# Expert layer of a decoder: weights as the stationary operand, rows added straight into the output

## The reference

```python
def moe(x, gate_w, w1, w3, w2):          # E = 8 experts, F = 512, TOPK = 2
    xt = x.reshape(b * s, d)             # 2048 tokens, d = 256
    logits = xt @ gate_w
    topv, topi = jax.lax.top_k(logits, TOPK)
    probs = jax.nn.softmax(topv, axis=-1)
    w = jnp.zeros_like(logits)
    for kk in range(TOPK):
        w = w + jax.nn.one_hot(topi[:, kk], E, dtype=logits.dtype) * probs[:, kk:kk + 1]
    out = jnp.zeros_like(xt)
    for e in range(E):
        h = jax.nn.silu(xt @ w1[e]) * (xt @ w3[e])
        out = out + w[:, e:e + 1] * (h @ w2[e])
    return out.reshape(b, s, d)

out = h + moe(rmsnorm(h, norm2_w), gate_w, w1, w3, w2)
```

## Time and profile before

| | us |
|---|---|
| median of 3 runs | 1277.4 (1275.44 to 1280.86) |
| the profiled execution's own time | 1279.25 |
| its span | 1277.2 |
| busy in the span: TensorE matmul / weight loads | 1159.9 / 816.0 |
| VectorE / ScalarE / GpSimd | 775.9 / 573.4 / 604.1 |
| expert stage, first row load to end | 1025.06 to 1277.2 |

### The profile page before, as it was taken

How to read it: one execution, slowest core, us unless ns; L and a number is a source line. 1 busy time by engine, 2 the same in 40 slices (tenths; PEclk the granted TensorE clock), 3 DMA queues, 4 the chain that set the end, 5 groups by cost and what they waited for, 6 DMA issues and landing times. The chain is left out here.

```text
span 1277.2 us, 24562 instructions
## 1 busy us (share of the span) xinstructions
PE 1159.9 (91%) x7393; PEld 816.0 (64%) x7394; DVE 775.9 (61%) x1914; ACT 573.4 (45%) x1505; POOL 604.1 (47%) x752
## 2 busy tenths in 40 slices
PE   7998889879999699789999999999999579999995
PEld 5785566545555344368888888888888346666663
DVE  5565788868888599755676767776766412222221
ACT  3444766633333100056666566666665223333331
POOL 2003556526555466456666556666655213223232
PEclk9999999989999899899999999999999789999998
DMA  7000000009992030140000000000003012222223
GB/s 275 0 1 9 18 14 12 9 2 205 203 198 59 15 157 1 70 198 1 9 14 14 22 13 12 12 12 16 13 22 145 31 36 43 48 41 46 44 45 86
DMA packets 46372, 69.43 MB, mean 54 GB/s; under 512 B 4609, under 2 KB 42817, under 8 KB 45249
## 3 DMA queue, kind: packets, MB, share of 16 engines
q1 hardware_dynamic: 37152, 52.95, 15.5%
q0 software_dynamic: 7152, 9.34, 4.5%
q10 hardware_dynamic: 2000, 6.29, 1.3%
HBM read 57.12 MB, written 32.58 MB: 70 GB/s over the span
## 5 line engine op out<-in xcount | busy, mean ns | idle before, releaser
L1926 PE MATMUL ga.pkq<-ga.xnT,g.early 128*128 128x128 f32 x1280 | 156.8, 276 | 1.0 <-ACT ga.halves L1844 1.0
L1926 PEld LDWEIGHTS ga.pkq<-ga.xnT,g.early 128*128 128x128 f32 x1280 | 151.4, 193 | 9.6 <-issue 8.2
L1703 POOL TENSOR_TENSOR ga.halves<-ga.halves,g.ga_sinT 128x512 f32<-128x512 f32 x80 | 103.1, 1288 | 53.1 <-ACT ga.halves L1844 53.1
L1970 PE MATMUL ga.turn_out<-g.early,ga.aT 128*128 128x256 f32 x512 | 117.0, 382 | 0.5 <-ACT ga.aT L1866 0.5
L1851 ACT ACTIVATE ga.e<-ga.psc,ga.negmax 128x128 f32<-128x128 f32 x256 | 90.6, 366 | 48.6 <-DVE ga.negmax L1772 47.7
L1711 POOL TENSOR_TENSOR ga.kqT<-ga.by_cos,ga.halves 128x512 f32<-128x512 f32 x80 | 102.3, 1279 | 15.9 <-issue 15.9
L1970 PEld LDWEIGHTS ga.turn_out<-g.early,ga.aT 128*128 128x128 f32 x512 | 94.9, 190 | 12.3 <-ACT ga.aT L1866 0.7
L2081 DVE TENSOR_TENSOR ex.hidden<-ex.silu,ex.p 128x512 f32<-128x512 f32 x39 | 26.8, 688 | 123.6 <-PE ex.p L2134 117.2
L1759 DVE TENSOR_TENSOR ga.by_cos<-ga.pkq,g.ga_cosT 128x512 f32<-128x512 f32 x80 | 55.3, 691 | 74.2 <-PE ga.pkq L1926 43.2
L2058 POOL TENSOR_TENSOR ex.token<-ex.token_d,ex.zero 128x1 uint32<-128x1 uint32 x39 | 7.0, 180 | 154.2 <-DVE ex.y L2087 143.5
L1951 PE MATMUL ga.paT<-ga.pT,ga.v 128*128 128x512 f32 x128 | 69.2, 623 | 11.8 <-ACT ga.pT L1859 9.1
(11 more groups left out here) (292 smaller groups left out, 2623.9 us busy)
## 6 DMA issues: line engine op xcount, KB each, us to landing
mo_rows<-in_pad_rows SPq DMA_DIRECT2D x1, 18447.0 KB, 100.8
ex.row<-mo_rows SPq DMA_DIRECT2D x39, 129.0 KB, 2.0
g.spare<-in_mo_w SPq DMA_DIRECT2D x1, 4096.0 KB, 12.2
g.late<-in_mo_w SPq DMA_DIRECT2D x1, 4096.0 KB, 21.9
g.early<-in_mo_w SPq DMA_DIRECT2D x1, 4096.0 KB, 12.6
g.ctxT<-in_ctxR SPq DMA_DIRECT2D x1, 2048.0 KB, 13.2
xa.ctxT<-in_ctxT SPq DMA_DIRECT2D x16, 128.0 KB, 2.5
g.spare<-cv_rows SPq DMA_DIRECT2D x1, 2048.0 KB, 9.7
```

What stands on the lines that cost most here:

```text
L1703: nc.gpsimd.tensor_tensor(by_sin[:, par, :].rearrange("p (h t) -> p h t", h=REP), halves[:, par, :].rearrange("p (h t) -> p h t", h=REP), ...
L1926: last = nc.tensor.matmul(pkq[:, par, j * P:(j + 1) * P], w[:, q, at * P:(at + 1) * P], xnT[:, s.par, q, :], start=(q == 0), stop=(q == C ...
L1970: last = nc.tensor.matmul(pout, aT[:, h // REP, (h % REP) * P:(h % REP + 1) * P], g.ga_wo[:, h, :], start=(h == 0), stop=(h == H - 1))
```

## The change

In the experts the operands of p1 and p3 change sides. The weights become stationary and the rows xnT move, so that p1 and p3 come out transposed, as four blocks of 128 hidden channels by 128 tokens in the columns of one bank; each is eight matmuls with 128 moving columns. The stationary operand isn't addressed by a register: ScalarE copies w1 of the expert of tile t+2, and VectorE w3, into buffers of their own (`w1`, `w3`, two each, 128x1024), by a register load of the expert's number on each engine. The product of silu and p3 is written as hT at once, in two buffers. The hidden transposes, their bank and ScalarE's hT copy go, and so does the register load ahead of p1. ScalarE and VectorE begin two tiles ahead instead of one (`steps(..., 2, 1)`), and wait once for the weights to be loaded.

The kernel's output tensor gets 128 rows more (for the padding rows) and takes the place of `mo_acc`: the router's sums are stored into it, the scatter adds into it, and the copy at the end goes. The padding rows are cut off after the kernel.

```diff
-        silu, hidden = m.sb("silu", [P, F]), m.sb("hidden", [P, F])
-        hT = m.sb("hT", [P, F])
+        silu, hT = m.sb("silu", [P, F]), m.sb("hT", [P, 2, F])
+        w1, w3 = m.sb("w1", [P, 2, C * F]), m.sb("w3", [P, 2, C * F])
...
@@ sync @@
             sp.wait_ge(added, 16 * TILES)
-            sp.dma_start(g.out.rearrange("b t d -> (b t d)").rearrange("(p n) -> p n", p=P),
-                         g.acc[0:B * P, :].rearrange("t d -> (t d)").rearrange("(p n) -> p n", p=P)).then_inc(out_stored, 16)
-            sp.wait_ge(out_stored, 16)
@@ vector @@
             def step(t):
+                if t.base is None and t.n == -2:
+                    dve.wait_ge(g.mo_loaded, 16 * g.mo_loads)
                 if t.on:
                     dve.wait_ge(silu_ready, upto(t))
                     dve.wait_ge(h3_done, upto(t))
-                    if t.past(1):
-                        dve.wait_ge(h_turned, upto(t, back=1))
-                    nc.vector.tensor_tensor(hidden[:], silu[:], p3[:], ALU.mult).then_inc(hidden_ready, 1)
+                    if t.past(2):
+                        dve.wait_ge(y_done, upto(t, back=2))
+                    nc.vector.tensor_tensor(hT[:, t.par, :], silu[:], p3[:], ALU.mult).then_inc(hT_ready, 1)
+                n = t.back(-2)
+                if n.on:
+                    expert = dve.value_load(g.tile_expert[0:1, bass.ds(n.i, 1)], min_val=0, max_val=E - 1)
+                    nc.vector.tensor_copy(w3[:, n.par, :], g.mo_w3[:, bass.ds(expert, 1), :, :].rearrange("p e c f -> p (e c f)")).then_inc(w3_ready, 1)
                 b = t.back(1)
...
@@ scalar @@
                     if t.past(1):
-                        act.wait_ge(hidden_ready, upto(t, back=1))
+                        act.wait_ge(hT_ready, upto(t, back=1))
                     nc.scalar.activation(silu[:], p1[:], ACT.Silu).then_inc(silu_ready, 1)
+                n = t.back(-2)
+                if n.on:
+                    expert = act.value_load(g.tile_expert[0:1, bass.ds(n.i, 1)], min_val=0, max_val=E - 1)
+                    nc.scalar.activation(w1[:, n.par, :], g.mo_w1[:, bass.ds(expert, 1), :, :].rearrange("p e c f -> p (e c f)"), ACT.Copy).then_inc(w1_ready, 1)
                 n = t.back(-1)
...
-                if t.on:
-                    act.wait_ge(h_turned, upto(t))
-                    if t.past(1):
-                        act.wait_ge(y_done, upto(t, back=1))
-                    nc.scalar.activation(hT[:], phT[:], ACT.Copy).then_inc(hT_ready, 1)
@@ tensor @@
                 if t.on:
-                    expert = pe.value_load(g.tile_expert[0:1, bass.ds(t.i, 1)], min_val=0, max_val=E - 1)
                     pe.wait_ge(xnT_ready, upto(t))
+                    pe.wait_ge(w1_ready, upto(t))
                     if t.past(1):
                         pe.wait_ge(silu_ready, upto(t, back=1))
-                    for c in range(C):
-                        last = nc.tensor.matmul(p1[:], xnT[:, t.par, c, :], g.mo_w1[:, bass.ds(expert, 1), c, :].rearrange("p e f -> p (e f)"), start=(c == 0), stop=(c == C - 1))
+                    for f in range(4):
+                        for c in range(C):
+                            last = nc.tensor.matmul(p1[:, f * P:(f + 1) * P], w1[:, t.par, c * F + f * P:c * F + (f + 1) * P], xnT[:, t.par, c, :], start=(c == 0), stop=(c == C - 1))
                     last.then_inc(h1_done, 1)
+                    pe.wait_ge(w3_ready, upto(t))
                     if t.past(1):
-                        pe.wait_ge(hidden_ready, upto(t, back=1))
+                        pe.wait_ge(hT_ready, upto(t, back=1))
...
-                if t.on:
-                    pe.wait_ge(hidden_ready, upto(t))
-                    if t.past(1):
-                        pe.wait_ge(hT_ready, upto(t, back=1))
-                    for f in range(4):
-                        last = nc.tensor.transpose(phT[:, f * P:(f + 1) * P], hidden[:, f * P:(f + 1) * P], g.ident[:])
-                    last.then_inc(h_turned, 1)
@@ decoder, kernel @@
-        g.h, g.out = h, out
+        g.h, g.acc = h, out
...
-    out = nc.dram_tensor("out_0", (B, P, D), F32, kind="ExternalOutput").ap()
+    out = nc.dram_tensor("out_0", (B * P + P, D), F32, kind="ExternalOutput").ap()
...
-    return r.results[0]["out_0"]
+    return r.results[0]["out_0"][0:B * P].reshape(B, P, D)
```

More of the change, by code:

```diff
@@ L1411, in allocate_moe @@
     g.rows = nc.dram_tensor("mo_rows", [E * REGION + SPARE * P, ROW], F32, kind="Internal").ap()
-    g.acc = nc.dram_tensor("mo_acc", [B * P + P, D], F32, kind="Internal").ap()
     g.tile_expert, g.tile_row = m.sb("tile_expert", [P, TILES], I32), m.sb("tile_row", [P, TILES], I32)
@@ L2015, in experts @@
         xnT = m.sb("xnT", [P, 2, C, P])
-        silu, hidden = m.sb("silu", [P, F]), m.sb("hidden", [P, F])
-        hT = m.sb("hT", [P, F])
+        silu, hT = m.sb("silu", [P, F]), m.sb("hT", [P, 2, F])
+        w1, w3 = m.sb("w1", [P, 2, C * F]), m.sb("w3", [P, 2, C * F])
         y = m.sb("y", [P, 2, D])
[L2019 to L2023, removed]
+        turn, p1, p3, py = m.ps("turn", [P, 512]), m.ps("p1", [P, F]), m.ps("p3", [P, F]), m.ps("py", [P, 512])
+        (meta_ready, token_ready, turned, xnT_ready, w1_ready, w3_ready, h1_done, h3_done, silu_ready, hT_ready, y_done, y_ready,
+         added) = map(m.sem, (
+            "meta_ready", "token_ready", "turned", "xnT_ready", "w1_ready", "w3_ready", "h1_done", "h3_done", "silu_ready", "hT_ready",
+            "y_done", "y_ready", "added"))
         row_loaded = [m.sem(f"row_loaded{i}") for i in range(2)]
@@ L2092, in step @@
                     meta(n)
-            steps(dve, step, 1, 1, count=TILES)
+            steps(dve, step, 2, 1, count=TILES)
         @block.scalar
@@ L2097, in step @@
             def step(t):
+                if t.base is None and t.n == -2:
+                    act.wait_ge(g.mo_loaded, 16 * g.mo_loads)
                 if t.on:
@@ L2110, in step @@
                     last.then_inc(xnT_ready, 1)
-                if t.on:
-                    act.wait_ge(h_turned, upto(t))
-                    if t.past(1):
-                        act.wait_ge(y_done, upto(t, back=1))
-                    nc.scalar.activation(hT[:], phT[:], ACT.Copy).then_inc(hT_ready, 1)
-            steps(act, step, 1, 1, count=TILES)
+            steps(act, step, 2, 1, count=TILES)
         @block.tensor
@@ L2123, in step @@
                 if t.on:
-                    expert = pe.value_load(g.tile_expert[0:1, bass.ds(t.i, 1)], min_val=0, max_val=E - 1)
                     pe.wait_ge(xnT_ready, upto(t))
+                    pe.wait_ge(w1_ready, upto(t))
                     if t.past(1):
                         pe.wait_ge(silu_ready, upto(t, back=1))
-                    for c in range(C):
-                        last = nc.tensor.matmul(p1[:], xnT[:, t.par, c, :], g.mo_w1[:, bass.ds(expert, 1), c, :].rearrange("p e f -> p (e f)"), start=(c == 0), stop=(c == C - 1))
+                    for f in range(4):
+                        for c in range(C):
+                            last = nc.tensor.matmul(p1[:, f * P:(f + 1) * P], w1[:, t.par, c * F + f * P:c * F + (f + 1) * P], xnT[:, t.par, c, :], start=(c == 0), stop=(c == C - 1))
                     last.then_inc(h1_done, 1)
+                    pe.wait_ge(w3_ready, upto(t))
                     if t.past(1):
-                        pe.wait_ge(hidden_ready, upto(t, back=1))
-                    for c in range(C):
-                        last = nc.tensor.matmul(p3[:], xnT[:, t.par, c, :], g.mo_w3[:, bass.ds(expert, 1), c, :].rearrange("p e f -> p (e f)"), start=(c == 0), stop=(c == C - 1))
+                        pe.wait_ge(hT_ready, upto(t, back=1))
+                    for f in range(4):
+                        for c in range(C):
+                            last = nc.tensor.matmul(p3[:, f * P:(f + 1) * P], w3[:, t.par, c * F + f * P:c * F + (f + 1) * P], xnT[:, t.par, c, :], start=(c == 0), stop=(c == C - 1))
                     last.then_inc(h3_done, 1)
@@ L2150, in step @@
                     for f in range(4):
-                        last = nc.tensor.matmul(py[:, 0:D], hT[:, f * P:(f + 1) * P], g.mo_w2[:, bass.ds(expert, 1), f, :].rearrange("p e d -> p (e d)"), start=(f == 0), stop=(f == 3))
+                        last = nc.tensor.matmul(py[:, 0:D], hT[:, b.par, f * P:(f + 1) * P], g.mo_w2[:, bass.ds(expert, 1), f, :].rearrange("p e d -> p (e d)"), start=(f == 0), stop=(f == 3))
                     last.then_inc(y_done, 1)
-                if t.on:
-                    pe.wait_ge(hidden_ready, upto(t))
-                    if t.past(1):
-                        pe.wait_ge(hT_ready, upto(t, back=1))
-                    for f in range(4):
-                        last = nc.tensor.transpose(phT[:, f * P:(f + 1) * P], hidden[:, f * P:(f + 1) * P], g.ident[:])
-                    last.then_inc(h_turned, 1)
             steps(pe, step, 1, 1, count=TILES)
```

## The result

The changed kernel takes 1258.56 us (median of 4 runs, 1257.11 to 1259.13) where the kernel before takes 1276.94 beside it: ratio 0.9851, 95% interval 0.9832 to 0.9869. Forecast were 1256.6 us and a range of 1251 to 1268. A second series, run later with the experiments (e4), gave 1257.43 against 1277.93: 0.9836 (0.9823 to 0.9849). The gain is 18.4 us in the first series and 20.5 in the second, where 20.8 was forecast. The profiled execution took 1259.13 us, its span is 1257.1.

What follows compares the result with a forecast made beforehand. The prediction took TensorE's own stream to bound the turns and the output copy to bound the end. Savings of 10.5 + 0.75 + 1.15 + 8.4 = 20.8 us from the median 1277.4 gave 1256.6 us, range 1251 to 1268.

Steps and rivals of the forecast that it cites:

- point 1: TensorE's turn: p1 and p3 as 32 records of 0.1117 us, plus row transposes and py, sum 5.52 us.
- point 2: Expert-number load ahead of py on TensorE's sequencer: mostly covered by queued records, costing 0.08 us a turn.
- The rival of ample cover: TensorE's queue takes in more than 7 to 8 records, so the expert-number load costs nothing: 1253.6 us; chance 0.15.
- point 3: TensorE's loop jump, now behind py, and the dropped load for p1: the 0.14 us in every second turn goes.
- points 4 to 6: ScalarE's w1 copy (1.02 us), VectorE's w3 copy (at most about 1.22) and GpSimd's scatter chain: each cost 0.
- point 7: First turn, p1(0) to p1(1): 7.72 us becomes 6.97, saving 0.75 us.
- point 8: Last turn, p1(38) to py(38): 6.53 us becomes 5.38, saving 1.15 us.
- point 9: End of the span: the output copy goes and everything after it until 1277.2, saving 8.4 us.

Runs made afterwards that it cites:

- e4: The changed kernel unaltered, run once more beside the other experiments: 1257.43 us against 1277.93 for the kernel before, ratio 0.9836.
- e5: The changed kernel with one more load of the expert's number ahead of py on TensorE's sequencer: 1257.41 us, ratio 0.9845.
- e6: The changed kernel with three more loads of the expert's number ahead of py on TensorE's sequencer: 1305.41 us, ratio 1.0220.
- e7: The changed kernel with the w1 copy made twice on ScalarE, the second into a buffer nobody reads: 1257.93 us, ratio 0.9849.
- e8: The changed kernel with two banks for py instead of one: 1257.54 us, ratio 0.9846.
- e1: The kernel before with only the output tensor changed, rows added straight into it and no copy at the end: 1271.51 us, ratio 0.9954.
- e3: The changed kernel with GpSimd waiting for the last scatter's landing ahead of its closing drain: 1259.54 us, ratio 0.9851.
- e10: The changed kernel with a GpSimd drain in every turn, behind the token operation and ahead of the scatter: 1257.46 us, ratio 0.9838.
- e11: The changed kernel with a GpSimd drain in every turn at the head of the step, before the wait for the previous scatter: 1256.85 us, ratio 0.9827.

## Why the prediction was right, and where it was not

The time came out 2 us above the forecast and well inside the range; by the profiled executions the sum was 20.8 and the stage gave 20.6. That is closer than the working deserves, and luck: the turns gave 3.0 us more than forecast, the last turn 1.2 and the end 1.9 less, and the three nearly cancel.

- *Turn (point 1)*: right to the hundredth. 32 records at the attention stage's 0.112, transposes and py at their old price give 5.52, and 5.521 was measured. The weight loads lie beneath the matmuls at this shape in the new place too; laid end to end with the matmuls they would make a turn of over 11 us. The Trainium skill's rule that a load overlaps only with different row groups (TensorE: Matmul & The Clock Gate, "The mechanism"; the prediction names the section behind it) doesn't hold here: TensorE is busy for 204.28 of 204.28 us with all rows in use.
- *Expert number for py (point 2)*: wrong. I took 0.08 us a turn; there is none, 3.0 us in the sum. I read a depth of 7 to 8 records off the moment at which the sequencer turned to the next register load. In that turn the sequencer had been held: it stood ahead of the hidden transposes, waiting for the hidden product. In the turn whose row follows, the product ends at 1145.93 + 0.69 = 1146.62, and the sequencer's next work starts at 1146.7, with the loop's jump:

```profile
1145.93 0.69 DVE L2081 TENSOR_TENSOR ex.hidden<-ex.silu,ex.p 128x512 f32<-128x512 f32 x1 [2.93 <-PE ex.p L2134]
L77 PEldq ALU_OP  x1: 32/32/32, 1146.7 to 1146.7; - x1
L2124 PEldq TENSOR_LOAD <-g.tile_expert x1: 304/304/304, 1147.2 to 1147.2; - x1
```

  What bounded the lead was a wait, not the queue. The change removed that wait with the transposes; e5 and e6 measure a lead of 1.9 us, some 18 records, where the chain needs 0.9. The rival of ample cover (chance 0.15) was the true one, though not with a queue beyond reach: e6 reaches its end at 18 matmul records, each with a weight load. The Trainium skill gives a depth of 64 (same page, the table at its head); no run here shows more than these 36 entries, if a record and its load count as one each.
- *Loop jump (point 3)*: right. The 0.14 us in every second turn is gone. The same held sequencer explains it by the rows above: after the release it had the jump and the load to do, and its last register work for p1 starts at 1148.1, as does p1's first weight load (1148.11). In the next turn, without a jump, that work starts at 1153.7, and the weight load at 1153.92. It wasn't tested by itself.
- *ScalarE, VectorE, GpSimd (points 4 to 6)*: right. The w1 copy is 1.06 for 1.02, the w3 copy 0.69, near the low end; e7 shows that ScalarE's room was real and about 0.9 us.
- *First turn (point 7)*: 0.70 for 0.75. No row of the prediction shows that the clock is low there; the trace of before has a granted clock of 0.50 from 1028.65 to 1032.00 us.
- *Last turn (point 8)*: wrong, 1.15 forecast and -0.05 found. I forgot that the last py waits for y of tile 37 to leave the bank, and, worse, that TensorE's end doesn't set the end of the stage: the last scatter waits for the one before it to land. e8 removes the bank's wait and gains nothing.
- *End (point 9)*: 8.4 forecast, 6.5 found. "With it everything" was the mistake: GpSimd's drain had been covered by the copy and became what ends last, so that the span ends 5.7 us after the last scatter is issued and not "about 4". e1 shows it by itself, 6.4 us.

## What to carry to other kernels

Price a matmul by the distance between starts at its own shape, taken from wherever the kernel has it already; here that gave the new turn to 0.1%. Before reading an engine's lead off the trace, look whether its sequencer was held by a wait: a lead bounded by a wait says nothing of the queue. And when the last transfer is removed, list what ran beneath it, and follow the end through every chain, since the engine with the most work needn't be in it.

## What the runs showed of the hardware that was not expected

- GpSimd's drain after 39 indirect transfers without one between takes 3.25 us with all of them landed (e3), and 0.21 to 0.53 after one or two where no longer operation of GpSimd stands before it (the changed kernel, e10), with one exception of 1.45. Placed behind a scatter in flight it lasts until 3.9 us after the scatter's issue (e11).
- TensorE's sequencer can be about 18 float32 matmul records (1.9 us at 0.11) ahead of the array (the changed kernel, e5, e6); one load of a value from on-chip memory into a register, with its arithmetic and assertion, costs it some 0.7 to 0.75 us (e6: the loads start 0.7 us apart, and all four with what follows take 3.1).
